# Old state times gated keys and queries as one 128-column product in a chunked delta-rule kernel on Trainium2

## What is computed

```python
def step(S, x):
    qt, kt, vt, bt, gt = x
    S = S * jnp.exp(gt)[..., None, None]
    kv = jnp.einsum('bhk,ebhkv->ebhv', kt, S)
    delta = (vt[None] - kv) * bt[..., None]
    S = S + kt[None, :, :, :, None] * delta[..., None, :]
    ot = jnp.einsum('bhk,ebhkv->ebhv', qt * scale, S)
    return (S, ot)
```

## Time and profile before

| | |
|---|---|
| time, median of 3 runs | 869.64 us (866.48 to 873.55) |
| profiled execution, its own time | 871.51 us |
| span from first to last instruction in it | 869.7 us |
| PE busy | 795.5 us, 91% |
| DVE busy | 639.5 us, 74% |
| ACT busy | 312.0 us, 36% |
| POOL busy | 291.5 us, 34% |
| mean granted TensorE clock | 0.984 |

### The profile page before, as it was taken

How to read it: one execution, slowest core, us unless ns; L and a number is a source line. 1 busy time by engine, 2 the same in 40 slices (tenths; PEclk the granted TensorE clock), 3 DMA queues, 4 the chain that set the end, 5 groups by cost and what they waited for, 6 DMA issues and landing times.

```text
span 869.7 us, 23569 instructions
## 1 busy us (share of the span) xinstructions
PE 795.5 (91%) x10074; PEld 532.2 (61%) x10074; DVE 639.5 (74%) x1345; ACT 312.0 (36%) x547; POOL 291.5 (34%) x280
## 2 busy tenths in 40 slices
PE   2998999999999999999999986999998999997698
PEld 1454444444566667865444446888888888897343
DVE  6999999995888856535843647887787878783385
ACT  1231112210122230023654533656555555653342
POOL 5221110000111141000673335656655565561650
PEclk9998999999999999999999997999999999999899
DMA  8600000023000016000049643454545455521452
GB/s 244 200 0 1 0 2 1 0 49 72 1 1 0 2 47 221 0 1 1 5 132 394 263 119 101 131 133 133 164 122 142 126 137 144 133 65 40 128 174 71
DMA packets 74961, 80.46 MB, mean 93 GB/s; under 512 B 34453, under 2 KB 57671, under 8 KB 74854
## 3 DMA queue, kind: packets, MB, share of 16 engines
q1 hardware_dynamic: 69733, 57.78, 24.0%
q0 software_dynamic: 5120, 21.14, 6.7%
HBM read 54.44 MB, written 24.39 MB: 91 GB/s over the span
## 4 chain that ended last, share of the span: by engine, by line
PE 69%; DVE 23%; issue 4%; POOL 1%; ACT 1%; DMA 1%; SPq 1%; DVEq 0%; POOLq 0%; ACTq 0%
PE bank L786 14%; PE bank L869 8%; PE bank L894 4%; PE bank L1069 4%; PE bank L582 4%; DVE rows L1558 3%; PE bank L596 3%; DVE rows L1687 3%; DVE rows L1560 3%; PE bank L801 2%; PE bank L885 2%; PE bank L994 2%; PE bank L919 2%; PE bank L798 2%; PE bank L956 2%
## 5 line engine op out<-in xcount | busy, mean ns | idle before, releaser
L786 PE MATMUL bank<-W,xT 128*128 128x512 f32 x280 | 124.2, 596 | 0.7 <-ACT big L1148 0.7
L786 PEld LDWEIGHTS bank<-W,xT 128*128 128x128 f32 x280 | 52.0, 190 | 60.2 <-issue 58.4
L560 PE MATMUL bank<-W,xT 128*125 128x512 f32 x160 | 79.2, 609 | 0.0
L1387 POOL TENSOR_TENSOR cnt_r<-cnt_r,ident_sb 125x125 fp32r<-125x125 f32 x10 | 11.4, 1144 | 173.8 <-ACT cnt_r L1134 173.8
L582 PEld LDWEIGHTS bank<-rows 128*126 128x126 f16 x360 | 43.5, 135 | 34.7 <-issue 24.2
L1693 DVE TENSOR_SCALAR rows<-iota_sb,tC 128x625 f16<-128x625 f16 x180 | 56.2, 378 | 10.5 <-PE bank L582 10.5
L582 PE MATMUL bank<-rows 128*126 128x313 f16 x360 | 58.9, 299 | 4.2 <-DVE rows L1693 4.1
L1558 DVE TENSOR_SCALAR rows<-iota_sb,gbp 125x180 f16<-125x180 f16 x160 | 56.2, 351 | 0.0
L1560 DVE TENSOR_SCALAR rows<-iota_sb,gbp 125x180 f16<-125x180 f16 x160 | 50.3, 315 | 0.0
L570 PE MATMUL bank<-rows 125*128 125x360 f16 x160 | 42.7, 321 | 5.1 <-DVE rows L1560 3.3
L1236 ACT ACTIVATE tB<-bank 128x1024 f16<-128x1024 f32 x40 | 40.9, 1024 | 13.8 <-PE bank L919 6.9
(11 more groups left out here) (336 smaller groups left out, 1916.8 us busy)
## 6 DMA issues: line engine op xcount, KB each, us to landing
big<-qkv_slots SPq DMA_DIRECT2D x40, 256.0 KB, 3.6
rows<-step_rows SPq DMA_DIRECT2D x40, 128.0 KB, 3.1
rows<-gam_rows SPq DMA_DIRECT2D x40, 128.0 KB, 3.5
big<-qkv_slots SPq DMA_DIRECT2D x80, 64.0 KB, 2.7
big<-qkv_slots SPq DMA_DIRECT2D x40, 128.0 KB, 3.0
o_slots<-big SPq DMA_DIRECT2D x40, 128.0 KB, 2.9
x_all<-in_x SPq DMA_DIRECT2D x10, 224.0 KB
out<-tC SPq DMA_DIRECT2D x10, 224.0 KB
```

The source lines that it names most:

```text
L560: last = mm(dst, xT[:, k, t * P:(t + 1) * P], W[:, w, k, :], start=(k == 0), stop=(k == KC - 1 and bias is None))
L786: last = mm(bank[:, b0, :], xT[:, k, t * P:t * P + 128], W[:, w, k, :], start=(k == 0), stop=(k == KC - 1))
```

## The change

`old_keys` and the query half of `out_part` become one step. The weights of the projections are laid out on the host so that what was the "key" and the "query" tile hold, for even heads, key and query, and for odd heads, query and key. Key and query features of a unit lie side by side (kqF), POOL multiplies both at once by the decay (`decayed_features`, 128 x 1024 in one instruction), and PE `old_keys_and_queries(c)` multiplies 128 stationary columns (64 key and 64 query columns of a head) with the old state of that head: 8 products for each chunk, b = 0 into bank DA and b = 1 into bank DB. For b = 0 the keys' result lies on partitions 0 to 63 and the queries' on 64 to 127; for b = 1 the other way round. So `right_side` reads its two halves from two banks, with two DVE instructions on 64 partitions; `new_values(c)` (what is left of `out_part`) adds scores times z onto the queries' part in both banks; and `keep_o` is two ACT instructions on 64 partitions, which apply the factor 1/8 too.

Since DA and DB now hold the outputs, `state_part` writes to other banks (`state_bank`): for the even chunk of a unit the TTB bank that `features(h + 1)` of the same hop will overwrite, for the odd one an MB bank. `features` waits for `state_done` for that reason. `new_state` no longer waits for the output of the last chunk. `new_values` stands right behind `state_part` on PE, `keep_o(h, 0)` ahead of `keep_mt(h)` on ACT, and several waits are dropped or merged (`b_done` and `tm_done` into `level_ready`).

```diff
-        kF, qF = ([f[:, :, w, :] for f in kqF] for w in range(2))
-        kG = [[unit(xTu, 2 + 2 * p + s) for s in range(2)] for p in range(2)]
+        evenF, oddF = ([f[:, :, w, :] for f in kqF] for w in range(2))
+        kqG = [[buf[:, n * D:(n + 2) * D].rearrange("p (a w n) -> p a w n", w=2, n=CL) for n in (n0, n0 + 2)] for buf, n0 in ((Wu, 4), (xTu, 2))]
         AT = [unit(big, 21), xTu[:, 3 * (N + 3) + 1:3 * (N + 3) + 1 + D].rearrange("p (a n) -> p a n", n=CL)]
...
         MB, TB, TTB, DA, DB = (0, 1), (2, 4), (3, 5), 6, 7
+        OLD = (DA, DB)
+
+        def late_bank(t):
+
+            return (0, 2, 3)[t - LATE]
+
+        def state_bank(c):
+
+            return MB[c // 2 % 2] if c % 2 else TTB[(c // 2 + 1) % 2]
+
+        def half(b):
+
+            return slice(CL * b, CL * b + CL)
...
             def features(u):
                 s = u % 2
                 pe.wait_ge(qk_loaded[u % 2], 32 * (u // 2 + 1))
-                if u >= 2:
+                if u == 2:
                     pe.wait_ge(S["tt_done"], u - 1)
+                if u >= 3:
+                    pe.wait_ge(S["state_done"], 2 * (u - 3) + 1)
...
-                pe.wait_ge(S["qF_done"], u + 1)
+                pe.wait_ge(S["oddF_done"], u + 1)
                 for a in range(8):
-                    for b in range(2):
-                        q = slice(CL * b, CL * b + CL)
-                        last = mm(pair_of_banks(s, a)[q, :], kF[s][q, a, :], kqF[s][q, a, :, :].rearrange("p w n -> p (w n)"), start=True, stop=True)
+                    mm(pair_of_banks(s, a)[half(0), :], evenF[s][half(0), a, :], kqF[s][half(0), a, :, :], start=True, stop=True)
+                    last = mm(pair_of_banks(s, a)[half(1), :], oddF[s][half(1), a, :], kqF[s][half(1), a, ::-1, :], start=True, stop=True)
...
-            def old_keys(c):
+            def old_keys_and_queries(c):
                 u, c2 = c // 2, c % 2
-                if c2 == 0:
-                    pe.wait_ge(S["kg_done"], u + 1)
+                if c2 == 0 and u + 2 >= NSC:
+                    pe.wait_ge(S["kd_done"], u + 1)
+                if c and (c2 == 0 or u + 2 >= NSC):
+                    pe.wait_ge(S["o_done"], c)
                 pe.wait_ge(S["state_done"], c)
                 for j in range(HB):
                     for b in range(2):
-                        q = slice(CL * b, CL * b + CL)
-                        last = mm(bank[q, DA, j * DH:(j + 1) * DH], kG[u // 2 % 2][u % 2][q, c2 * HB + j, :], state[q, c % 2, j, :],
-                                  start=True, stop=True)
+                        last = mm(bank[:, OLD[b], j * DH:(j + 1) * DH], kqG[u // 2 % 2][u % 2][half(b), c2 * HB + j, :, :].rearrange("p w n -> p (w n)"),
+                                  state[half(b), c % 2, j, :], start=(j == 0), stop=True, skip_group_check=True)
                 last.then_inc(S["ks_psum"], 1)
 
             def solve(c):
                 u, c2 = c // 2, c % 2
-                if c2 == 0:
-                    pe.wait_ge(S["tf_done"], u + 1)
                 pe.wait_ge(S["y_ready"], c + 1)
                 for j in range(HB):
                     for b in range(2):
                         q = slice(CL * b, CL * b + CL)
                         last = mm(bank[q, DA, HW2 + j * DH:HW2 + (j + 1) * DH], TF[u // 2 % 2][u % 2][q, c2 * HB + j, :], yv[c % 2][q, j, :],
-                                  start=True, stop=True)
+                                  start=False, stop=True, skip_group_check=True)
                 last.then_inc(S["z_psum"], 1)
 
             def state_part(c):
                 u, c2 = c // 2, c % 2
-                if c2 == 0:
-                    pe.wait_ge(S["kd_done"], u + 1)
                 pe.wait_ge(S["z_done"], c + 1)
                 for j in range(HB):
                     for b in range(2):
                         q = slice(CL * b, CL * b + CL)
-                        last = mm(bank[q, DA, j * DH:(j + 1) * DH], kD[u // 2 % 2][u % 2][q, c2 * HB + j, :], zt[c % 2][q, j, :],
+                        last = mm(bank[q, state_bank(c), j * DH:(j + 1) * DH], kD[u // 2 % 2][u % 2][q, c2 * HB + j, :], zt[c % 2][q, j, :],
                                   start=True, stop=True)
                 last.then_inc(S["s_psum"], 1)
 
-            def out_part(c):
+            def new_values(c):
                 u, c2 = c // 2, c % 2
-                if c2 == 0:
-                    pe.wait_ge(S["qg_done"], u + 1)
-                if c:
-                    pe.wait_ge(S["o_done"], c)
-                o0 = c % 2 * HW2
+                pe.wait_ge(S["z_done"], c + 1)
                 for j in range(HB):
                     for b in range(2):
-                        q = slice(CL * b, CL * b + CL)
-                        mm(bank[q, DB, o0 + j * DH:o0 + (j + 1) * DH], qG[u // 2 % 2][u % 2][q, c2 * HB + j, :], state[q, c % 2, j, :],
-                           start=True, stop=False)
-                    for b in range(2):
-                        q = slice(CL * b, CL * b + CL)
-                        last = mm(bank[q, DB, o0 + j * DH:o0 + (j + 1) * DH], PT[u // 2 % 2][u % 2][q, c2 * HB + j, :], zt[c % 2][q, j, :],
-                                  start=False, stop=True)
+                        last = mm(bank[half(1 - b), OLD[b], j * DH:(j + 1) * DH], PT[u // 2 % 2][u % 2][half(b), c2 * HB + j, :], zt[c % 2][half(b), j, :],
+                                  start=False, stop=True, skip_group_check=True)
                 last.then_inc(S["o_psum"], 1)
...
-                chunk_of(old_keys, h, 0)
+                chunk_of(old_keys_and_queries, h, 0)
                 unit_of(last_level, h - 1)
-                if h >= 3:
-                    out_part(2 * (h - 3) + 1)
                 chunk_of(solve, h, 0)
                 unit_of(residual, h - 1)
                 unit_of(first_m, h)
                 chunk_of(state_part, h, 0)
+                chunk_of(new_values, h, 0)
                 unit_of(first_mt, h)
                 unit_of(features, h + 1)
                 unit_of(level_up, h, 1)
-                chunk_of(old_keys, h, 1)
+                chunk_of(old_keys_and_queries, h, 1)
                 unit_of(first_fix, h - 1)
                 unit_of(level_up, h, 2)
                 chunk_of(solve, h, 1)
                 unit_of(second_fix, h - 1)
-                chunk_of(out_part, h, 0)
                 chunk_of(state_part, h, 1)
-            out_part(NCK - 1)
+                chunk_of(new_values, h, 1)
...
             def keep_z(c):
                 act.wait_ge(S["z_psum"], c + 1)
-                if c >= 2:
-                    act.wait_ge(S["o_psum"], c - 1)
                 A(flat(zt[c % 2]), bank[:, DA, HW2:2 * HW2], ACT.Copy).then_inc(S["z_done"], 1)
...
-                A(ot[u % 2][:, c % 2, :], bank[:, DB, c % 2 * HW2:(c % 2 + 1) * HW2], ACT.Copy).then_inc(S["o_done"], 1)
+                for b in range(2):
+                    last = A(ot[u % 2][half(1 - b), c % 2, :], bank[half(1 - b), OLD[b], 0:HW2], ACT.Copy, scale=DH ** -0.5)
+                last.then_inc(S["o_done"], 1)
...
             for h in range(NSC + 2):
                 unit_of(keep_tm, h - 1, 3)
                 unit_of(keep_t, h - 1)
-                if h >= 3:
-                    keep_o(2 * (h - 3) + 1)
                 chunk_of(keep_z, h, 0)
+                unit_of(keep_residual, h - 1)
+                chunk_of(keep_o, h, 0)
                 unit_of(keep_mt, h)
-                unit_of(keep_residual, h - 1)
-                unit_of(key_features, h + 1)
+                unit_of(even_features, h + 1)
                 unit_of(keep_tm, h, 1)
-                unit_of(query_features, h + 1)
+                unit_of(odd_features, h + 1)
                 unit_of(keep_fix, h - 1)
                 chunk_of(keep_z, h, 1)
                 unit_of(keep_tm, h, 2)
-                chunk_of(keep_o, h, 0)
-            keep_o(NCK - 1)
+                chunk_of(keep_o, h, 1)
...
-            def decayed_keys(u):
+            def decayed_features(u):
                 s, p = u % 2, u // 2 % 2
                 pool.wait_ge(grow_loaded[u % 2], 32 * (u // 2 + 1))
-                pool.wait_ge(S["kF_done"], u + 1)
+                pool.wait_ge(S["evenF_done"], u + 1)
+                pool.wait_ge(S["oddF_done"], u + 1)
                 if u >= 4:
                     pool.wait_ge(S["ks_psum"], 2 * (u - 4) + 2)
-                G.tensor_tensor(kG[p][s], kF[s], grow[s], ALU.mult).then_inc(S["kg_done"], 1)
-
-            def decayed_queries(u):
-                s, p = u % 2, u // 2 % 2
-                pool.wait_ge(S["qF_done"], u + 1)
-                if u >= 4:
-                    pool.wait_ge(S["o_psum"], 2 * (u - 4) + 2)
-                G.tensor_tensor(qG[p][s], qF[s], grow[s], ALU.mult).then_inc(S["qg_done"], 1)
+                G.tensor_tensor(kqG[p][s], kqF[s], grow[s].unsqueeze(2).broadcast_to([128, 8, 2, CL]), ALU.mult).then_inc(S["kg_done"], 1)
...
```

(14 more changed lines are left out.)

80 lines of the change are left out of this document (36 added, 44 removed).

## The result

The changed kernel takes **912.73 us** (median of 6, 908.61 to 916.25) where the kernel before, timed beside it, takes 869.83 (median of 6): a ratio of 1.0483, 95% interval 1.0441 to 1.0526, 4.8% slower. The forecast was 889, and its range ended at 905.

What follows compares the result with a forecast made beforehand. PE was taken as the bound, other engines' latencies just covered. PE work 12.2 + waits 2.45 + packets 0.05 made 14.7 us a hop against 13.8: +16.4 over 18 hops, +3 at the end, 889 us; range 863 to 905.

Steps and rivals of the forecast that it cites:

- The walk: One loop hop followed from `level_up` 3 through PE, DVE and ACT in five numbered steps: 14.7 us against 13.8.
- five waits: PE waits before the even solve 0.5, `first_m` 0.4, `features` 0.75, odd `state_part` 0.4, `level_up` 3 0.4: 2.45 us a hop.
- 0.2 bound: Lower bound for each half of `right_side` on DVE, 0.2 us, from 64 x 160 copies taking 0.23; 0.75 for both was forecast.
- Loads queue: Rival: weight loads of the two partition halves go one after the other, each merged step 1.74 us; 924 us, 8%.
- cheap steps: Rival: merged product 0.46 us, or halves of 0.2 us on DVE; 880 or just below, 870 with both; 17%.
- faster: Rival: PE stays the bound; 848 us with the product at 0.46, 863 at 0.87 and no wait; 12%.
- +3: Last two hops, where nothing covers the chain: 4 chunks each longer by 0.41 (product) and 0.33 us (DVE's second half).
- step 1: Merged product from 2.23 to 3.10, DVE's `right_side` from 3.25 to 4.07; PE waits 0.5 us for `y_ready`.
- step 4: `features` to the odd chunk's `second_fix` on PE, then `state_part` needs `keep_z`: a wait of 0.4 us.
- steps 1, 2, 3 and 5: Step 2: DVE to the transpose, `first_m` waits 0.4 us; step 3: `features` waits 0.75 for `new_state(h, 0)`.
- step 5: Second merged product to `level_up` 3 through `right_side`, scan, mask, `keep_tm`: 3.86 us against 3.45 of PE work, wait 0.4.
- text packets: PE waiting for its own program text: 1.4 us a hop before, mostly arriving during other waits after, 0.05 left.

Runs made afterwards that it cites:

- e7: The kernel before with the changed order and with `right_side` and `keep_o` each split into two halves of 64 partitions: 894.52 us, ratio 1.0250.
- e1: The changed kernel with the merged step as sixteen 64 x 64 products in place of 8 with 128 columns: 903.39 us, ratio 1.0350.
- e12: The kernel before with only the levels' two semaphores merged into one: 860.30 us, ratio 0.9913.
- e16: The changed kernel with the levels' two counters of the kernel before in place of the merged one: 910.76 us, ratio 1.0483.
- e5: The kernel before with only the new order of the output step on PE and of `keep_o` on ACT: 876.72 us, ratio 1.0055.
- e4: The changed kernel with `right_side` as one DVE instruction on 128 partitions, wrong for odd heads, so only a price: 895.64 us, ratio 1.0281.

## Why the prediction was right or wrong

**Direction and mechanism held, but for one link.** PE was the bound with the other engines just covered, the change saves little PE time and takes the cover away. The walk did not have the link through POOL. All five waits that the walk named appear; four are in the waits above, and the one for `keep_z` shows as 0.48 us from `second_fix` (647.30) to `state_part` (647.78), where sixteen f16 products take 0.25. The largest is `features` behind `new_state`, as said (1.1, 0.75 forecast). The halves of `right_side` are 0.42 us each; their group on the page (busy, mean ns, idle before, releaser):

```profile
L1987 DVE TENSOR_TENSOR tC<-big,bank 64x256 f32<-64x256 f32 x80 | 33.5, 418 | 31.7 <-PE bank L968 31.1
```

Half the partitions do not halve the time, and the earlier trace rows's 0.2 bound was the wrong neighbour. The merged product's loads go side by side: its MATMULs start in pairs, 0.007 us apart, and the pairs 0.11 apart. "Loads queue" (924) and "cheap steps" (870 to 880) fall with these rows, and so does "faster".

**Where it was wrong: the size, +43 instead of +19.** The step that failed is the walk that gave 14.7 us for a hop: it put the cost of the merged step's edges at 0 and POOL's joint instruction at nothing, and took DVE's terms too short. The `+3` for the end of the loop failed beside it. The walk against the trace, start to start:

| from, to | walk | after | difference |
|---|---|---|---|
| `level_up` 3, first merged step | 2.23 | 2.09 | −0.14 |
| first merged step, `right_side` | 1.02 | 1.23 | +0.21 |
| `right_side`, `first_m` | 2.75 | 2.97 | +0.22 |
| `first_m`, `features` | 2.15 | 2.34 | +0.19 |
| `features`, second merged step | 1.87 | 1.81 | −0.06 |
| second merged step, `right_side` | 1.02 | 1.23 | +0.21 |
| `right_side`, `level_up` 3 | 3.71 | 3.99 | +0.28 |

The walk was 14.7 and the hop is 15.66. Measured, 17 hops are 32.7 us longer than before, where +0.9 a hop gives 15.5: some 17 us, of the 24 that the forecast missed by. (Two slips in the walk's own sums are too small to matter: step 1 gives `right_side` 0.82 where the text has 0.75, and the terms of step 4 make 0.33 for a wait put at 0.4.)

*The drain, taken as 0.* The pairs of the merged step start 0.11 us apart, which makes 0.89 for eight. But the second pair starts 0.16 behind the first and the next block 0.21 behind the last, so it is 1.04 us from the step's first start to the next block's (636.07 to 637.11, 644.42 to 645.46), and DVE is freed 1.23 us behind its start where the walk had 1.02. I had this as "0 in the sum, 0.25 in the range" and "partly inside waits". The Trainium skill ("TensorEngine Tiling (Array Packing)", Key Properties) says that a change of tiling mode drains; the trace agrees (0.16 and 0.21 at the edges for 0.11 inside), and it should have stood in the sum. The odd chunk's visit pays its 0.21 in full, 3.6 us in 17 hops. The even chunk's alone costs nothing more, because `lower16` would have to wait for `sources` just the same.

*POOL's joint instruction, taken as nothing.* I wrote that `sources`, "which it delays by 1.3 us, is not used until the scan at the end of the hop". Its result isn't. But it runs beside `lower16`, which takes 0.83 to 0.89 us in the changed kernel's hops for the 0.69 of the hop that I read; in twelve of seventeen hops of the kernel before it took 0.85 to 0.92 too, but there PE set the pace. That is 0.14 us a hop on top of the path through the merged step, some 2 us, and it takes away what a shorter step in the even half could give. What the joint instruction costs in all no run shows: none puts `decayed_features` apart again or behind `sources`.

*DVE's instructions one by one.* The terms of steps 1, 2, 3 and 5 were mis-sized in the same direction: I took lengths and spacings that had held between whole instructions of before. The walk had 2.70 from the start of `right_side` to the end of the transpose, and the trace has 2.91 (637.30 to 640.21), 0.14 of it the length of `lower16`; on to the end of `new_state` 2.25 (to 642.46) for 2.1, and `features` starts 0.15 behind that end where I had 0.05. In step 5 the scan starts 0.88 behind `right_side` where I had 0.75, and the mask 1.25 behind the scan for 1.14. None is large; the three stretches make 0.69 us a hop, `lower16` included, and with the 0.42 of the merged step's two visits, less the 0.20 by which two stretches came out shorter, they are the 0.91 of the table.

*The end of the loop, taken as +3.* Behind the last `features` the changed kernel loses 10.9 us in the profiled execution, 1.9 of them by the longer hop and 9 in the last two hops. In these the merged step waits for `o_done` of the chunk before, a link that the walk didn't have (PE in order of time, behind the last unit's levels):

```profile
830.77 1.11 PE L968 MATMUL bank<-state,xT 64*128 64x64 f32 x16 [1.48 <-ACT big L1263]
...
837.03 1.11 PE L968 MATMUL bank<-state,xT 64*128 64x64 f32 x16 [0.92 <-ACT big L1263]
...
843.09 1.97 PE L968 MATMUL bank<-state,xT 64*128 64x64 f32 x16 [0.87 <-ACT big L1263]
```

Old state times queries went straight into the bank that `keep_o` had still to read; before, `old_keys` used a bank of its own and only `out_part`, off the chain, waited. And PE, which is idle more in these hops, shows a lower granted clock. Two windows of the end, after (clock third from the end):

```profile
831.00:841.00 10.00, 7.59 (x152) 6.91 (x152) 2.79 (x6) 2.12 (x5) 0.61 (x1) 0.75 0.14 29
841.00:851.00 10.00, 7.63 (x96) 5.99 (x94) 1.68 (x4) 1.89 (x5) 0.61 (x1) 0.50 0.01 2
```

and one before, where this part of the work ran at the full 2.4 GHz:

```profile
794.00:804.00 10.00, 7.47 (x234) 6.84 (x232) 2.38 (x5) 2.41 (x6) 1.23 (x2) 1.00 0.14 30
```

At 1.2 GHz the merged step takes 1.97 us (843.09) for 1.11. From the last `features` to the first product behind the loop it is 38.9 us before, 39.8 in e7 and 49.8 after, with mean clocks of 1.00, 1.00 and 0.80: the order and the splits put only 1 us there, so the rest belongs to what e7 lacks, the wide step, its wait for `keep_o` and the clock. e1 has the same waits for `keep_o` (3.8 us in all, in both) and yet 43.3 us, with the narrow step and a clock of 0.87. How the 9 us divide between width, wait and clock was not separated. The clock's part differs from one execution to the next: of the changed kernel's six, the two with a mean clock of 0.983 take 908.6 us, the four with 0.974 to 0.976 take 912.7 to 916.3, and the profiled one is the longest.

*Waits merged, taken as nothing.* The step "waits dropped or merged" had no term at all. It holds a gain of 8 us in the kernel before (e12), and it made no error in the sum only because the loop, once bound by a chain, shows none of it (e16). That was luck. The 1.4 us of text packets a hop, which I let the waits swallow, did vanish from PE's waits.

**The range.** Its upper end, 905, took the drains in full and 10 us for short waits. The hops came out 17 us over the sum, about what these two allowed for, and the loop's end 7 over, for which the range had no room.

## What to carry to other kernels

When one engine is 92% busy and every other latency is "just covered", price a change by the cycle it closes, not by the work it saves: the order alone cost 4 us, a split alone 5, both 22. On such a cycle put every known edge cost in the sum, drains and gaps between instructions included, look at what the engine that is "loosely loaded" runs beside each link (POOL, busy 34%, held DVE's `lower16`), and walk the last iterations separately, for what nothing covers there and for buffers that two steps now share. And test the bookkeeping of waits by itself: the only gain of this change was there (0.9% alone, 1.2% with six more waits gone), and it needed none of the rest. Last, read the hops one by one: a mean of 15.53 us hid twelve hops of 15.15 and four of 16.7.

## What the runs showed of the hardware

- A step of eight 64 x 128 products between 64 x 64 ones costs 1.04 us to the next start and frees its reader 1.23 us behind its own start. The same work as sixteen 64 x 64 products, the four of a head pair on four quarters of the array, costs 0.52 and 0.84 (e1, 822.66 us).
- Two DVE instructions on 64 partitions x 256 take 0.85 us, one on 128 takes 0.41 (0.42 in e5's order). The instruction behind the two starts 0.87 to 0.88 us behind the first of them, the one behind a single one 0.33: the split costs 0.54 in issue, not 0.41.
- A DVE `tensor_tensor` with both inputs in SBUF (`lower16`, 0.69 us alone) that starts while POOL's `sources` runs ends 0.55 us behind the end of `sources`: 0.83 us in the changed kernel, 1.28 in e1, 1.38 in e4.
- The granted clock can fall inside the loop too: in four of e1's sixteen hops `features` took 1.69 to 1.94 us for 1.06 with the clock at 1.2 GHz, behind a wait that every hop has, and each such hop was 1.4 to 1.6 us longer. What sets it off these rows don't say.
- PE's losses at its program text (15.6 us in fifteen hops) changed with how it waits: 11.4 when each level waits for one semaphore instead of two, none to be seen when the loop is bound by a chain. Four waits a unit that are always met cost 0.3% (0.1 to 0.5).
